# Cross-attention and routed feed-forward: the last step of odd batches on GpSimd, first roots for four batches at once, and a later normalisation

## The chip, the cores and the metric

The kernel runs on one core of one Trainium2 chip. The metric is the device time of one execution in microseconds (us). Its engines are called here by their names and, in rows of the profile, PE (TensorE), PEld (TensorE's weight loads), DVE (VectorE), ACT (ScalarE), POOL (GpSimd) and SP (SyncE, the DMA queue).

## The reference, cut to what matters

x and ctx are 128 batches of 128 rows by 256 columns, float32.

```python
def reference(x, ctx, Wq, bq, Wkv, bkv, Wo, bo, w_router, w_block):
    h = layernorm(x)                                   # (x - m) / sqrt(v + 1e-5), over 256 columns
    q, k, v = h @ Wq + bq, ctx @ Wkv[:, :256] + bkv[:256], ctx @ Wkv[:, 256:] + bkv[256:]
    attn = softmax(q_h @ k_h.T / 4)                    # 16 heads of 16
    x1 = x + (attn @ v_h) @ Wo + bo
    z = layernorm(x1)
    top = top_k(z @ w_router, 96 of 128 rows)          # in each batch
    u = z;  u[top] = gelu(z[top] @ w_block)            # the other rows keep z
    return x1 + u
```

## The kernel before, in words

One batch (128 x 256, rows on the partitions) is the unit of work. After a prologue each engine runs a hand-written loop over s, and one pass ("slot s") works on several batches at different stages. The engines are tied by semaphores only: each executes its list in program order, and a wait holds everything behind it on that engine. Four engines carry one list each.

TensorE in slot s (functions of the same names): `scores(s)` (L329), `transpose_inputs(s + 5)` (L358, of the normalised x, `xhat`, and of ctx), `values(s - 1)` and the queries or keys of a pair (both through L287), the router's two small transposes once in eight slots (`candidates` L473 where s = 4 mod 8, `keep_columns` L480 where s = 0 mod 8), `projection(s - 2)` (L294), a wait for `xhat` of batch s + 6, `block_product(s - 4)` (L294), then a wait for `v_pad` of batch s - 1 (`scaled_values_ready`), `transpose_x1(s - 3)` (L374) and `attention(s - 1)` (L394). In slots 20 to 119 the wait for `v_pad` stands ahead of `transpose_x1`.

ScalarE in slot s: `attention_copy(s - 2)`, `gelu_tanh(s - 7)`, `inputs_high(s + 5)` (L569), and the 16 exponentials of batch s (L558).

VectorE in slot s: the copy of transposed x1, the statistics of both norms (L705, L710, L694, L699), the four maxima (L671), `values_and_bias` (L764), `inputs_low` (L723), `inverse_sums(s - 1)` (L716, it makes `recip`), queries or keys and their bias, `residual` (L688), the router's steps (L791 to L813, in five of eight slots), `final(s - 16)` (L829) and `product_scaled(s - 4)` (L776). `final` is the last step of a batch: z_sb = z_sb * half_keep + x1_sb, where z_sb holds twice the gelu, half_keep is 0.5 for kept rows and 0 for the others, and x1_sb already holds what x1 + u has beside the gelu (`unprocessed`).

GpSimd in slot s, in this order: `normalise(s + 7)` (L984), `rstd1_of_pair(s + 9)` in odd slots (L972 variance + eps, L973 negated mean, L975 power -0.5) or `rstd2_of_pair(s - 4)` in even slots (L1015, L1017), `gelu_square(s - 5)` (L1033), `values_over_sums(s - 1)` (L1004, it makes `v_pad` and waits for `recip`), `scale_and_shift` once in eight slots (L1072, L1073), `unprocessed(s - 16)` (L1082), `gelu_factor(s - 5)` (L1043), `gelu_sum(s - 7)` (L1057), `input_and_bias(s + 4)` (L993), `gelu_cubic(s - 5)` (L1050) and `gelu_product(s - 7)` (L1064).

SP in slot s: in odd slots the eight q_eo transfers of a pair, the store of a pair (`store(s - 17)`, when both finals are done) and `load_x(s + 13)`; in even slots `load_c(s + 8)`.

x, x1 and z are kept in rings of 16 batches, `xhat` and the gelu's intermediate in rings of four. The last batches run through an epilogue written out by hand. The order of GpSimd's loop is:

```python
            for s in range(4, B):
                sure = 20 <= s < B - 1
                normalise(s + 7, sure)
                rstd1_of_pair(s + 9)
                rstd2_of_pair(s - 4)
                gelu_square(s - 5, sure)
                values_over_sums(s - 1, sure)
```

## Time and profile before

| | |
|---|---|
| median of 3 runs | 929.75 us (929.29 to 930.64) |
| the profiled execution | 928.47 us, span 926.7 us |
| granted TensorE clock, mean | 0.986 of full speed |
| TensorE, weight loads | busy 891.2 us (96%), 756.0 us (82%) |
| VectorE | busy 872.8 us (94%) |
| ScalarE | busy 876.0 us (95%) |
| GpSimd | busy 796.2 us (86%) |
| DMA | 25.8% of the span of 16 engines |

The page gives busy time and, for each group of instructions, how long the engine idled before it and what ended the wait. The timeline gives single instructions: start, length, engine, line, tiles written and read, and in brackets the idle time before with its releaser. Numbers in tile names are left out there, so x_sb stands for x_sb and x1_sb, rstd for rstd1 and rstd2, and so on. Instructions on one engine can overlap their neighbours by some hundredths, so what one costs its queue is best read from its start to the next start.

### The profile page before, as it was taken

To read this page: it belongs to the slowest core of one execution; us is meant where nothing else is said; L and a number is where in the kernel's file an instruction comes from. 1 tells how busy PE (TensorE), PEld (TensorE's weight loads), DVE (VectorE), ACT (ScalarE), POOL (GpSimd) and SP (SyncE) were. 2 spreads that over 40 slices of the span, in tenths; PEclk is the share of its full clock that TensorE was granted. 3 is DMA by queue.
4 is the path that set the end of the run, shared out by engine and by line. 5 is a ranking of instruction groups with operands and counts; after the bars stand their busy time and mean duration, and the time that the engine had idled before them with its cause. 6 is when DMAs were issued, how large, how long until landed. Compare 5 with 4: busy or idle time off the path is not lost. (4 is left out here: it accounts for less than half of the span.)

```text
span 926.7 us, 30985 instructions
## 1 busy us (share of the span) xinstructions
PE 891.2 (96%) x10296; PEld 756.0 (82%) x10296; DVE 872.8 (94%) x2318; ACT 876.0 (95%) x4499; POOL 796.2 (86%) x1488
## 2 busy tenths in 40 slices
PE   6899999999999999999999999999999999999972
PEld 5688888888888888888888888888888888888861
DVE  4799999999999999999999999999999999999887
ACT  2899999999999999999999999999999999999983
POOL 4367879999999999899999989999999999998865
PEclk7999999999999999999999999999999999999997
DMA  5312222222232232232232223223223223221102
GB/s 171 90 50 62 67 65 59 87 76 72 86 93 56 84 92 59 84 92 63 81 89 74 73 87 93 55 86 92 58 84 92 64 79 89 72 63 53 48 23 92
DMA packets 71232, 70.71 MB, mean 76 GB/s; under 512 B 12192, under 2 KB 62880, under 8 KB 71072
## 3 DMA queue, kind: packets, MB, share of 16 engines
q1 hardware_dynamic: 71072, 68.73, 25.8%
q8 instruction: 82, 1.34, 0.6%
q14 instruction: 78, 0.64, 0.2%
HBM read 35.13 MB, written 16.78 MB: 56 GB/s over the span
## 5 line engine op out<-in xcount | busy, mean ns | idle before, releaser
L558 ACT ACTIVATE e_sb<-ps_s,neg_max 128x128 f32<-128x128 f32 x2048 | 717.1, 409 | 8.5 <-DVE neg_max L671 7.9
L558 ACT ACTIVATION_READ_ACCUMULATOR e_sb<-ps_s,neg_max 128x1 f32 x2048 | 511.1, 250 | 0.0
L671 DVE TENSOR_REDUCE neg_max<-ps_s 128x4 f32<-128x512 f32 x512 | 328.9, 663 | 32.6 <-PE ps_s L329 32.6
L329 PE MATMUL ps_s<-q_eo,k_sb 32*128 32x256 f32 x2048 | 147.6, 402 | 6.1 <-DMA q_eo<-q_raw 3.7
L394 PE MATMUL ps_a<-e_sb,v_pad 128*32 128x128 f32 x4096 | 138.4, 276 | 2.2 <-DVE x_sb L688 1.6
L294 PE MATMUL ps_a<-w_o_sb,o_sb 128*128 128x256 f32 x512 | 133.2, 382 | 2.0 <-DVE v_sb L764 1.9
L294 PE MATMUL ps_t<-w_z_sb,xt_sb 128*128 128x258 f32 x512 | 132.7, 381 | 1.3 <-DVE z_sb L776 1.3
L1004 POOL TENSOR_TENSOR v_pad<-v_sb,recip 128x256 f32<-128x256 f32 x128 | 79.4, 621 | 58.9 <-DVE recip L716 54.4
L394 PEld LDWEIGHTS ps_a<-e_sb,v_pad 128*32 128x32 f32 x4096 | 104.1, 109 | 24.0 <-issue 21.5
L329 PEld LDWEIGHTS ps_s<-q_eo,k_sb 32*128 32x128 f32 x2048 | 93.0, 185 | 34.6 <-ACT e_sb L558 18.8
L993 POOL TENSOR_TENSOR x_sb<-x_sb,bo_sb 128x256 f32<-128x256 f32 x128 | 114.7, 897 | 0.2
L294 PEld LDWEIGHTS ps_t<-w_z_sb,xt_sb 128*128 128x128 f32 x512 | 97.3, 191 | 15.3 <-issue 1.8
L294 PEld LDWEIGHTS ps_a<-w_o_sb,o_sb 128*128 128x128 f32 x512 | 88.2, 189 | 10.0 <-issue 2.5
L569 ACT CAST t_hi<-ps_t 128x512 fp32r<-128x512 f32 x127 | 74.5, 587 | 20.9 <-PE ps_t L358 15.9
L1050 POOL TENSOR_TENSOR g_sb<-g_sb,z_sb 128x256 f32<-128x256 f32 x128 | 90.7, 708 | 0.3
L723 DVE TENSOR_TENSOR t_lo<-ps_t,t_hi 128x512 fp32r<-128x512 f32 x127 | 85.9, 676 | 0.9 <-ACT t_hi L569 0.7
L287 PE MATMUL ps_a<-w_v_hi,t_hi 128*128 128x256 f32 x256 | 83.9, 328 | 1.7 <-ACT o_sb L577 1.5
L1064 POOL TENSOR_TENSOR z_sb<-g_sb,z_sb 128x256 f32<-128x256 f32 x121 | 82.5, 682 | 0.0
L287 PE MATMUL ps_q<-t_hi,w_q_hi 128*128 128x256 f32 x256 | 73.6, 288 | 4.0 <-DVE t_lo L723 2.4
L1033 POOL TENSOR_TENSOR g_sb<-z_sb 128x256 f32<-128x256 f32 x123 | 75.3, 612 | 0.3 <-DVE z_sb L776 0.3
L287 PE MATMUL ps_q<-t_hi,w_q_lo 128*128 128x256 f32 x256 | 73.1, 285 | 0.0
L287 PE MATMUL ps_q<-t_lo,w_q_hi 128*128 128x256 f32 x256 | 73.1, 285 | 0.0
(92 smaller groups left out, 2195.1 us busy)
## 6 DMA issues: line engine op xcount, KB each, us to landing
x_sb<-in_x SPq DMA_DIRECT2D x64, 256.0 KB, 3.0
c_sb<-in_ctx SPq DMA_DIRECT2D x64, 256.0 KB, 3.2
q_eo<-q_raw SPq DMA_DIRECT2D x512, 32.0 KB, 2.0
out<-z_sb SPq DMA_DIRECT2D x64, 256.0 KB, 2.4
z_sb<-in_L_xattn_Wkv SPq DMA_DIRECT2D x2, 256.0 KB, 5.3
...
```

The lines of the kernel that those rows point to most:

```text
L287: last = nc.tensor.matmul(dst, lhs(a, c), rhs(b, c), start=(c == 0 and n == 0), stop=(c == C - 1 and n == len(terms) - 1))
L294: last = nc.tensor.matmul(dst, lhs(c), rhs(c), start=(c == 0), stop=(c == C - 1))
L329: mm = nc.tensor.matmul(ps_s[:, bank(b, j), c, :, :], k_sb[rows, r2, c, h * T:(h + 1) * T], q_eo[rows, r2, :, c, h, :], start=True, stop=True)
L394: mm = nc.tensor.matmul(ps_attn[32 * j:32 * j + 32, c * T:(c + 1) * T], v_pad[:, b % 2, c * J + j, par:par + 2, :].rearrange("p a d -> p ( ...
L558: last = nc.scalar.activation(e_sb[:, b % 4, j, c, par, :], ps_s[:, bank(b, j), c, par, :], ACT.Exp, bias=neg_max[:, b % 4, h:h + 1], accu ...
L671: nc.vector.tensor_reduce(neg_max[:, b % 4, :].rearrange("p (c j q) -> p j c q", c=C, j=J)[:, j, :, :], ps_s[:, bank(b, j), :, :, :], AX.X ...
L723: nc.vector.tensor_tensor(t_lo[part].rearrange("p k c t -> p (k c) t"), inputs_bank(b)[:, :].rearrange("p (n t) -> p n t", t=T), t_hi[part ...
L993: nc.gpsimd.tensor_tensor(x_sb[:, b % R, :], x_sb[:, b % R, :], bo_sb[:, :], ALU.add).then_inc(xb_ready, 1)
L1004: nc.gpsimd.tensor_tensor(v_pad[:, b % 2, :, 0:3:2, :], v_sb[:, b % 2, :].rearrange("p (g q d) -> p g q d", q=2, d=D), recip[:, b % 4, :]. ...
L1033: nc.gpsimd.tensor_tensor(g_sb[:, b % 4, :], z_sb[:, b % R, 0:E], z_sb[:, b % R, 0:E], ALU.mult).then_inc(square_ready, 1)
L1050: nc.gpsimd.tensor_tensor(g_sb[:, b % 4, :], g_sb[:, b % 4, :], z_sb[:, b % R, 0:E], ALU.mult).then_inc(cubic_ready, 1)
L1064: nc.gpsimd.tensor_tensor(z_sb[:, b % R, 0:E], g_sb[:, b % 4, :], z_sb[:, b % R, 0:E], ALU.mult).then_inc(gelu_ready, 1)
```

## The change

There are three edits, all of them about GpSimd's list.

1. `final` of the odd batches 5 to 111 (54 of them) leaves VectorE. GpSimd does it in two steps in slot b + 16: `final_scaled` multiplies z_sb by the column half_keep, and four steps later `final_sum` adds x1_sb. The store of a pair waits for both engines.
2. First roots (1 / sqrt(variance + eps) of x) are taken for four batches at once from batch 16 on: `variance1` ahead of `values_over_sums` and `root1` behind it, in slots 9, 13, 17, ..., 117. Before, it was two batches in every odd slot.
3. `normalise` subtracts the mean as it stands, so that the negation is dropped, and it works on batch s + 6 in place of s + 7.

```diff
@@ sb tiles @@
-        eps_sb = sb("eps_sb", [P, 2])
-        minus_half = sb("minus_half", [P, 2])
+        eps_sb = sb("eps_sb", [P, 4])
+        minus_half = sb("minus_half", [P, 4])
-        neg_m1 = sb("neg_m1", [P, R])
...
+        FINAL_ON_POOL = tuple(range(5, B - 16, 2))
+
+        def finals_on_pool(b):
+            return sum(1 for n in FINAL_ON_POOL if n <= b)
@@ SP, store @@
-                    sp.wait_ge(final_ready, upto(b + 1))
+                    sp.wait_ge(final_ready, upto(b + 1) - finals_on_pool(b + 1))
+                    if b + 1 in FINAL_ON_POOL:
+                        sp.wait_ge(final_pool_ready, finals_on_pool(b + 1))
@@ VectorE, final @@
-                if has(b):
+                if has(b) and b not in FINAL_ON_POOL:
@@ GpSimd @@
+            def final_scaled(b):
+
+                if b in FINAL_ON_POOL:
+                    g, k, r = (b // GROUP) % 2, b % GROUP, b % R
+                    nc.gpsimd.tensor_scalar(z_sb[:, r, 0:E], z_sb[:, r, 0:E], half_keep[:, g, k:k + 1], None,
+                                            ALU.mult).then_inc(scaled_ready, 1)
+
+            def final_sum(b):
+
+                if b in FINAL_ON_POOL:
+                    pool.wait_ge(u_ready, upto(b))
+                    pool.wait_ge(scaled_ready, finals_on_pool(b))
+                    nc.gpsimd.tensor_tensor(z_sb[:, b % R, 0:E], z_sb[:, b % R, 0:E], x1_sb[:, b % R, :],
+                                            ALU.add).then_inc(final_pool_ready, 1)
+
+            def variance1(b, n):
+
+                if b % n == 0 and has(b):
+                    r = slice(b % R, b % R + n)
+                    pool.wait_ge(mv1_ready, upto(b + n - 1))
+                    nc.gpsimd.tensor_tensor(ve1[:, r], mv1[:, r, 1], eps_sb[:, 0:n], ALU.add).then_inc(ve1_ready, n)
+
+            def root1(b, n):
+
+                if b % n == 0 and has(b):
+                    r = slice(b % R, b % R + n)
+                    pool.wait_ge(ve1_ready, upto(b + n - 1))
+                    nc.gpsimd.tensor_tensor(rstd1[:, r], ve1[:, r], minus_half[:, 0:n], ALU.pow).then_inc(rstd1_ready, n)
+
             def rstd1_of_pair(b):
...
+                variance1(b, 2)
+                root1(b, 2)
...
-                    nc.gpsimd.tensor_scalar(xhat[:, b % 4, :], x_sb[:, r, :], neg_m1[:, r:r + 1], rstd1[:, r:r + 1],
-                                            ALU.add, ALU.mult).then_inc(xhat_ready, 1)
+                    nc.gpsimd.tensor_scalar(xhat[:, b % 4, :], x_sb[:, r, :], mv1[:, r, 0:1], rstd1[:, r:r + 1],
+                                            ALU.subtract, ALU.mult).then_inc(xhat_ready, 1)
...
-            normalise(10)
-
             for s in range(4, B):
                 sure = 20 <= s < B - 1
-                normalise(s + 7, sure)
-                rstd1_of_pair(s + 9)
+                normalise(s + 6, sure)
                 rstd2_of_pair(s - 4)
                 gelu_square(s - 5, sure)
+                if s == 5:
+                    variance1(14, 2)
+                if s >= 9:
+                    variance1(s + 7, 4)
                 values_over_sums(s - 1, sure)
+                if s == 5:
+                    root1(14, 2)
+                if s >= 9:
+                    root1(s + 7, 4)
                 scale_and_shift(s - 16)
                 unprocessed(s - 16, sure)
                 gelu_factor(s - 5)
+                final_scaled(s - 16)
                 gelu_sum(s - 7)
                 input_and_bias(s + 4)
                 gelu_cubic(s - 5)
+                final_sum(s - 16)
                 gelu_product(s - 7)
```

GpSimd's list from `v_pad` of slot 65 on, before (x1_sb is the residual, g_sb the gelu's intermediate, ve2 and rstd2 the second root):

```order
L1004 TENSOR_TENSOR v_pad<-v_sb,recip 128x8x2x16 [waits recip_ready]
L1082 TENSOR_SCALAR x1_sb<-x1_sb,alpha,beta 128x256 [waits beta_ready]
L1043 TENSOR_SCALAR g_sb<-g_sb 128x256 [waits square_ready]
L1057 TENSOR_SCALAR g_sb<-g_sb 128x256 [waits tanh_ready]
L993 TENSOR_TENSOR x_sb<-x_sb,bo_sb 128x256 [waits xhat_ready]
L1050 TENSOR_TENSOR g_sb<-g_sb,z_sb 128x256 [waits factor_ready]
L1064 TENSOR_TENSOR z_sb<-g_sb,z_sb 128x256 [waits gelu_sum_ready]
L984 TENSOR_SCALAR xhat<-x_sb,neg_m1,rstd1 128x256 [waits rstd1_r]
L1015 TENSOR_TENSOR ve2<-mv2,eps_sb 128x2 [waits mv2_r]
L1017 TENSOR_TENSOR rstd2<-ve2,minus_half 128x2 [waits ve2_r]
L1033 TENSOR_TENSOR g_sb<-z_sb 128x256 [waits z_ready]
L1004 TENSOR_TENSOR v_pad<-v_sb,recip 128x8x2x16 [waits recip_ready]
```

The same place now (the last two rows above, square and next `v_pad`, follow behind L1048, the second root's power):

```order
L1035 TENSOR_TENSOR v_pad<-v_sb,recip 128x8x2x16 [waits recip_ready]
L1001 TENSOR_TENSOR rstd1<-ve1,minus_half 128x4 [waits ve1_r]
L1113 TENSOR_SCALAR x1_sb<-x1_sb,alpha,beta 128x256 [waits beta_ready]
L1074 TENSOR_SCALAR g_sb<-g_sb 128x256 [waits square_ready]
L978 TENSOR_SCALAR z_sb<-z_sb,half_keep 128x256
L1088 TENSOR_SCALAR g_sb<-g_sb 128x256 [waits tanh_ready]
L1024 TENSOR_TENSOR x_sb<-x_sb,bo_sb 128x256 [waits xhat_ready]
L1081 TENSOR_TENSOR g_sb<-g_sb,z_sb 128x256 [waits factor_ready]
L986 TENSOR_TENSOR z_sb<-z_sb,x1_sb 128x256 [waits scaled_ready,u_ready]
L1095 TENSOR_TENSOR z_sb<-g_sb,z_sb 128x256 [waits gelu_sum_ready]
L1015 TENSOR_SCALAR xhat<-x_sb,mv1,rstd1 128x256 [waits rstd1_r]
L1046 TENSOR_TENSOR ve2<-mv2,eps_sb 128x2 [waits mv2_r]
```

Three instructions are new between the two `v_pad`: L1001 (only where s = 1 mod 4), L978 and L986 (in every odd slot from 21 on).

TensorE's list around the wait for `v_pad` in slot 66 is the same before and after; here it is of the change (L301 is `block_product`, L381 `transpose_x1`, L401 `attention`, L336 the next `scores`):

```order
L301 MATMUL ps_t<-w_z_sb,xt_sb 128x258 [waits t_lo_ready,c_in4,xhat_ready]
L301 MATMUL ps_t<-w_z_sb,xt_sb 128x258
L381 MATMUL ps_q<-ident,x1_sb 128x128 [waits k_ready,v_pad_ready]
L381 MATMUL ps_q<-ident,x1_sb 128x128
L401 MATMUL ps_a<-e_sb,v_pad 32x128 [waits x1_ready]
L401 MATMUL ps_a<-e_sb,v_pad 32x128 x15
L336 MATMUL ps_s<-q_eo,k_sb 128x256 [waits exp_ready1]
```

The wait for `v_pad_ready` stands at the transpose of x1, ahead of attention and of the next scores. On VectorE the list of an odd slot is as before without L829.

## Rows read from the trace of the kernel before

**Rows 1.** The page, part 1: busy time, share of the span, instructions.

```profile
PE 891.2 (96%) x10296; PEld 756.0 (82%) x10296; DVE 872.8 (94%) x2318; ACT 876.0 (95%) x4499; POOL 796.2 (86%) x1488
```

**Rows 2.** Timeline, TensorE's weight loads: start us, length us, what, [idle before, releaser].

```profile
469.36 0.74 PEld L329 LDWEIGHTS ps_s<-q_eo,k_sb 32*128 32x128 f32 x16 [0.20 <-issue]
...
476.13 0.74 PEld L329 LDWEIGHTS ps_s<-q_eo,k_sb 32*128 32x128 f32 x16 [0.20 <-ACT e_sb L558]
...
481.38 0.36 PEld L374 LDWEIGHTS ps_q<-ident,x_sb 128*128 128x128 f32 x2
...
482.92 0.74 PEld L329 LDWEIGHTS ps_s<-q_eo,k_sb 32*128 32x128 f32 x16 [0.20 <-ACT e_sb L558]
...
524.15 0.74 PEld L329 LDWEIGHTS ps_s<-q_eo,k_sb 32*128 32x128 f32 x16 [0.20 <-issue]
```

**Rows 3.** Timeline of an early slot: weight loads of the scores, and v_pad on GpSimd.

```profile
85.54 0.74 PEld L329 LDWEIGHTS ps_s<-q_eo,k_sb 32*128 32x128 f32 x16 [0.20 <-ACT e_sb L558]
...
92.32 0.74 PEld L329 LDWEIGHTS ps_s<-q_eo,k_sb 32*128 32x128 f32 x16 [0.20 <-ACT e_sb L558]
...
89.30 0.62 POOL L1004 TENSOR_TENSOR v_pad<-v_sb,recip 128x256 f32<-128x256 f32 x1 [1.16 <-DVE recip L716]
```

**Rows 4.** Timeline, VectorE in slots 65 and 66.

```profile
475.07 0.48 DVE L829 SCALAR_TENSOR_TENSOR z_sb<-z_sb,half_keep,x_sb 128x256 f32<-128x256 f32 x1
475.47 0.42 DVE L694 BATCH_NORM_STATS2 st<-x_sb 128x6 f32<-128x256 f32 x1
...
477.42 1.29 DVE L671 TENSOR_REDUCE neg_max<-ps_s 128x4 f32<-128x512 f32 x2 [0.27 <-PE ps_s L329]
...
479.57 0.24 DVE L716 RECIPROCAL recip<-sums 128x16 f32<-128x16 f32 x1
```

**Rows 5.** Timeline, GpSimd from v_pad of slot 65 to v_pad of slot 66.

```profile
473.11 0.62 POOL L1004 TENSOR_TENSOR v_pad<-v_sb,recip 128x256 f32<-128x256 f32 x1
473.72 0.56 POOL L1082 TENSOR_SCALAR x_sb<-x_sb,alpha,beta 128x256 f32<-128x256 f32 x1
474.35 0.40 POOL L1043 TENSOR_SCALAR g_sb<-g_sb 128x256 f32<-128x256 f32 x1
...
475.20 0.94 POOL L993 TENSOR_TENSOR x_sb<-x_sb,bo_sb 128x256 f32<-128x256 f32 x1
476.11 0.72 POOL L1050 TENSOR_TENSOR g_sb<-g_sb,z_sb 128x256 f32<-128x256 f32 x1
...
477.51 0.55 POOL L984 TENSOR_SCALAR xhat<-x_sb,neg_m,rstd 128x256 f32<-128x256 f32 x1
478.04 0.18 POOL L1015 TENSOR_TENSOR ve<-mv,eps_sb 128x2 f32<-128x2 f32 x1
478.36 0.70 POOL L1017 TENSOR_TENSOR rstd<-ve,minus_half 128x2 f32<-128x2 f32 x1
479.03 0.61 POOL L1033 TENSOR_TENSOR g_sb<-z_sb 128x256 f32<-128x256 f32 x1
479.89 0.62 POOL L1004 TENSOR_TENSOR v_pad<-v_sb,recip 128x256 f32<-128x256 f32 x1 [0.25 <-DVE recip L716]
```

**Rows 6.** Timeline, weight loads of the scores of slots 70 and 71.

```profile
503.37 0.31 PEld L329 LDWEIGHTS ps_s<-q_eo,k_sb 32*128 32x128 f32 x8 [0.20 <-ACT e_sb L558]
...
510.25 0.53 PEld L329 LDWEIGHTS ps_s<-q_eo,k_sb 32*128 32x128 f32 x12 [0.20 <-issue]
```

**Rows 7.** Timeline, GpSimd: the bias sum of slot 68.

```profile
495.56 0.73 POOL L993 TENSOR_TENSOR x_sb<-x_sb,bo_sb 128x256 f32<-128x256 f32 x1
```

**Rows 8.** Timeline, GpSimd: first roots and v_pad of slot 67.

```profile
484.63 0.19 POOL L972 TENSOR_TENSOR ve<-mv,eps_sb 128x2 f32<-128x2 f32 x1
...
485.66 0.61 POOL L1033 TENSOR_TENSOR g_sb<-z_sb 128x256 f32<-128x256 f32 x1
486.67 0.62 POOL L1004 TENSOR_TENSOR v_pad<-v_sb,recip 128x256 f32<-128x256 f32 x1 [0.41 <-DVE recip L716]
```

**Rows 9.** Timeline, GpSimd near the end: the power of one column.

```profile
909.38 0.56 POOL L1024 TENSOR_TENSOR rstd<-ve,minus_half 128x1 f32<-128x1 f32 x1
```

More of the change, by code:

```diff
@@ L193, in cross_attention_routed_ffn @@
         final_ready = sem("final_ready")
+        scaled_ready, final_pool_ready = sem("scaled_ready"), sem("final_pool_ready")
         block = ctx.enter_context(nc.Block())
@@ L965, in _ @@
             pool.wait_ge(v_pad_zero, 1)
-            def rstd1_of_pair(b):
-                if b % 2 == 0 and has(b):
-                    r = slice(b % R, b % R + 2)
-                    pool.wait_ge(mv1_ready, upto(b + 1))
-                    nc.gpsimd.tensor_tensor(ve1[:, r], mv1[:, r, 1], eps_sb[:, :], ALU.add).then_inc(ve1_ready, 2)
-                    nc.gpsimd.tensor_scalar(neg_m1[:, r], mv1[:, r, 0], -1.0, None, ALU.mult)
-                    pool.wait_ge(ve1_ready, upto(b + 1))
-                    nc.gpsimd.tensor_tensor(rstd1[:, r], ve1[:, r], minus_half[:, :], ALU.pow).then_inc(rstd1_ready, 2)
+            def final_scaled(b):
[19 more added lines that the diff above has]
+                    nc.gpsimd.tensor_tensor(rstd1[:, r], ve1[:, r], minus_half[:, 0:n], ALU.pow).then_inc(rstd1_ready, n)
+            def rstd1_of_pair(b):
+                variance1(b, 2)
+                root1(b, 2)
             def normalise(b, settled=False):
@@ L1014, in rstd2_of_pair @@
                     pool.wait_ge(mv2_ready, upto(b + 1))
-                    nc.gpsimd.tensor_tensor(ve2[:, r], mv2[:, r, 1], eps_sb[:, :], ALU.add).then_inc(ve2_ready, 2)
+                    nc.gpsimd.tensor_tensor(ve2[:, r], mv2[:, r, 1], eps_sb[:, 0:2], ALU.add).then_inc(ve2_ready, 2)
                     pool.wait_ge(ve2_ready, upto(b + 1))
-                    nc.gpsimd.tensor_tensor(rstd2[:, r], ve2[:, r], minus_half[:, :], ALU.pow).then_inc(rstd2_ready, 2)
+                    nc.gpsimd.tensor_tensor(rstd2[:, r], ve2[:, r], minus_half[:, 0:2], ALU.pow).then_inc(rstd2_ready, 2)
             def rstd2_of_one(b):
```

## The prediction, made before the changed kernel ran

> **What bounds the kernel now.** I read the busy shares first. Four engines are busy for 86% to 96% of the span [rows 1], so a share alone decides nothing. The question is which engine has no slack in the main loop, where one batch takes one pass ("slot") s. I then followed TensorE's weight loads from one first score product (L329) to the next: an ordinary slot is 6.77 to 6.79 us (469.36, 476.13, 482.92), and the eight slots to 524.15 take 54.79 [rows 2]. A bubble of 0.20 us stands ahead of the scores in every slot, whoever is named as its releaser.
>
> The proof that this pace is TensorE's own stands in the early slots. From 85.54 to 92.32, before any final step or router is running on VectorE, the slot is 6.78 too, and GpSimd sits idle 1.16 us in it ahead of v_pad [rows 3]. So slack on GpSimd and VectorE buys nothing below 6.78. In slot 66 VectorE idles as well, 0.27 us until the scores come [rows 4].
>
> GpSimd is next, since the change loads it. Its queue from v_pad of slot 65 to v_pad of slot 66 takes 479.89 - 473.11 = 6.78 us, of which 0.25 is idle, until VectorE's reciprocal [rows 5]. So it works 6.53 us. The even v_pad ends at 479.89 + 0.62 = 480.51. TensorE's transpose of x1 (L374), which must wait for it, starts at 481.38 [rows 2], 0.87 us later. A release takes about 0.08 us: the reciprocal ended at 479.57 + 0.24 = 479.81 [rows 4], v_pad began at 479.89. **So v_pad of an even slot may start 0.79 us later than it does, and no more**: a stretch from odd to even v_pad may be 6.78 + 0.79 = 7.57 us long. What is queued behind that wait on TensorE (attention, the next scores, the next transposes) moves with it one to one.
>
> **The change, part by part.**
>
> *VectorE loses 54 final steps* (batches 5 to 111, odd). One costs 475.47 - 475.07 = 0.40 us of its queue [rows 4]. VectorE isn't the bound, so this gives only what its lateness costs TensorE. I find one such place, behind the router's steps: slot 70 is 510.25 - 503.37 = 6.88 long, 0.10 above the ordinary [rows 6]. I credit it whole: 13 groups of eight x 0.10 = **-1.3 us**. The bounds are 0, and all that eight slots hold above eight ordinary ones, 54.79 - 8 x 6.78 = 0.55, that is 7.2 us; the rest of it is where TensorE has the router's two small products, so I leave it out.
>
> *GpSimd, odd slots: two steps more.* final_scaled reads one tensor and one column per partition. The nearest rows are tensor_scalar steps: 0.40 us with constants (L1043), 0.53 to the next start for normalise (L984), 0.63 for the shift (L1082) [rows 5]. I take 0.53, the same kind of operands, with the others as bounds. final_sum adds two tensors of 256, like L1050 and L1064, which take 477.51 - 476.11 = 1.40 together [rows 5]. I take 0.70, bounds 0.61 (v_pad, 473.11 to 473.72) and 0.72.
>
> *What the missing final gives back.* In this slot the bias sum L993 takes 0.94 us, begun at 475.20 while VectorE's final (two SBUF inputs) runs from 475.07; where GpSimd was first it took 0.73 [rows 4, 5, 7]. Without the final: -0.21.
>
> *GpSimd, first roots.* Gone from every odd slot are sum, negation and power, 485.66 - 484.63 = 1.03 us [rows 8]. They stood ahead of an odd v_pad, in the stretch from even to odd. In their place one slot in four has a four-column sum ahead of v_pad (0.18 like the two-column one, L1015) and **a four-column power behind v_pad, in an odd slot, so in the stretch to the tight even one**. The power took 0.70 us for two columns [rows 5] and 0.56 for one [rows 9], 0.14 a column: four are an estimated 0.98, and 0.95 to the next start, as two took 0.67 (478.36 to 479.03). Bounds: 0.67 (no dearer than two columns) and 1.37 (two of them).
>
> *The stretches.* Odd to even without the root: 6.53 - 0.21 + 0.53 + 0.70 = 7.55 us, which just fits in 7.57. With the root: 7.55 + 0.95 = 8.50, which is 0.93 too long. So in slots 22, 26, ... TensorE waits 0.93 us for v_pad. There are 25 (root and final in one slot: s = 21, 25, ..., 117): 25 x 0.93 = **+23.3 us**.
>
> *Does it catch up?* Even to odd the work was 486.67 - 479.89 - 0.41 = 6.37 and becomes 6.37 - 1.03 + 0.18 = 5.52 [rows 5, 8]. After its wait TensorE takes 1.54 us to the next scores (481.38 to 482.92), and from these to the next v_pad it is 3.75 (482.92 to 486.67) [rows 2, 8]. So the odd v_pad comes 0.62 + 0.08 + 1.54 + 3.75 = 5.99 us after the even one and GpSimd idles 0.47 before it. Its lateness ends there, but TensorE has no slack to regain its own. The idle time merely moves ahead of the odd v_pad, where it helps nobody.
>
> *Normalise a slot later.* TensorE asks for it before the block product, but on GpSimd it stands ahead of second root and square, 1.6 us before v_pad even starts, and v_pad is wanted next, at L374. So v_pad is always the later of the two. Cost 0; the cover is this order. If it went, the wait would move to the block product and not grow. Subtracting the mean is the same instruction with another operand: 0.
>
> *Stores.* An odd batch's last step now ends late in GpSimd's slot, so SP issues the store of a pair up to some 4 us later, and the load of x behind it. That load is used three slots (20 us) on, and z_sb is wanted again three slots on. Next on SP are a load of ctx used four slots on and the q_eo transfers of two slots on. Cost 0; without that cover a late landing would cost its lateness once in two slots.
>
> *The end.* GpSimd finishes slot 127 about 1.2 us later and then waits for VectorE's statistics as now: 0.
>
> **Sum.** +23.3 - 1.3 = +22.0 on the profiled execution's 928.47 us gives 950.5. The median of the runs is 1.28 above that execution (929.75), so the forecast is **951.8 us**. All bounds low: 6.32 + 0.40 + 0.61 + 0.67 = 8.00, 0.43 too long, 25 x 0.43 - 1.3 = +9.5, 939 us. All high: 9.04, 1.47 too long, and the 29 stretches without a root 0.10 too long, +38, 968 us.
>
> The Trainium skill ("GPSIMD Engine Reference", 4.1 Engine selection) sends elementwise work to VectorE and puts GpSimd at about twice its time for two-input steps. This speaks against the change; the rows here are harsher, since one step of 0.40 becomes two of together 1.23.
>
> **Rivals.**
> *Cheaper steps on GpSimd.* The two final steps together take twice VectorE's 0.40, that is 0.80, the power as estimated. The stretch is 6.32 + 0.80 + 0.95 = 8.07, the wait 0.50, the sum 12.5 - 1.3 = +11.2, **941 us**. For it: an unseen step with one column may run at L1043's 0.40. Against: final_sum alone has rows near 0.70. (It is the time that the factor of two of the page named above would give.)
> *Faster: the stretch fits.* If final_scaled, final_sum and the power stay under 7.57 - 6.32 = 1.25 us together, or TensorE does not in truth stop at L374, only VectorE's relief is left, 1.3 to 7.2 us, middle 4.3: **925.5 us**. For it: slots behind the router are longer, so VectorE does reach TensorE. Against: the low ends of the rows sum to 1.68 already, and the early slots show the pace without that load.
> *Nothing measurable.* The steps are cheap and the waits vanish in TensorE's bubbles (0.20 ahead of the scores): about 930. Against: these bubbles stand in every slot, waiting or not.
> *Much slower.* Power in proportion to columns and a dear final_scaled, so that stretches without a root overrun too: **968 us**. For it: those fit by 0.02 us only.
>
> **Chances.** Forecast (943 to 966) 0.66; cheaper steps 0.14; faster 0.08; nothing measurable 0.06; much slower 0.06. The likeliest gives the time. The range 931 to 966 takes in the first two and leaves out 0.20. A measurement of this kernel can tell about 0.2% (1.9 us) from no change: faster 0.08, same 0.06, slower 0.86.
>
> **What would show it.** In the profile after: TensorE waiting about 0.9 us for v_pad ahead of the transpose of x1 in slots 22, 26, ..., 25 times, and hardly elsewhere; a slot of about 7.7 us there and 6.78 beside it; the four-column power near 0.98 us, final_scaled near 0.55, final_sum near 0.72, the bias sum 0.73 in odd slots; GpSimd idle about 0.5 us ahead of odd v_pads and not ahead of even ones; VectorE idle more. The forecast is wrong if the even v_pad behind a root still waits for the reciprocal, or if the slots of 6.78 get shorter.

## The result, and the profile after

The changed kernel takes **1011.51 us** (median of 4 runs, 1009.19 to 1013.08). The kernel before, run beside it, takes 929.52 (928.34 to 930.64, 4 runs). The ratio is 1.0886, with an interval of 1.0865 to 1.0907. It is slower, as predicted, but by 82.0 us where 22 were forecast and 38 were the dearest case thought of.

The profiled execution took 1013.08 us, with a span of 1011.2. First the page's busy times, which answer to [rows 1]:

```profile
PE 917.6 (91%) x10296; PEld 756.3 (75%) x10296; DVE 858.7 (85%) x2264; ACT 880.3 (87%) x4499; POOL 920.9 (91%) x1476
```

GpSimd has 124.7 us more work than before (920.9 against 796.2). The prediction gave it far less: 54 x (0.53 + 0.70 - 0.21) = 55 us for the final steps, and less work for the first roots. So the question is which instructions hold the rest. The groups of instructions on GpSimd, shapes apart (line, operation, tiles, shapes, count | busy us, mean ns | idle before them):

```profile
L1015 POOL TENSOR_SCALAR xhat<-x_sb,mv,rstd 128x256 f32<-128x256 f32 x128 | 157.0, 1227 | 0.4
...
L978 POOL TENSOR_SCALAR z_sb<-z_sb,half_keep 128x256 f32<-128x256 f32 x54 | 50.3, 931 | 5.1
...
L986 POOL TENSOR_TENSOR z_sb<-z_sb,x_sb 128x256 f32<-128x256 f32 x54 | 34.5, 639 | 0.0
L1001 POOL TENSOR_TENSOR rstd<-ve,minus_half 128x4 f32<-128x4 f32 x28 | 28.8, 1028 | 0.0
```

`normalise` (L1015) takes 1.23 us; before it took 0.55 [rows 5, L984]. The prediction had its new operand at nothing and did not price its new operation. That is 128 x 0.68 = 87 us of GpSimd's time. `final_scaled` (L978) takes 0.93, against 0.53 forecast and 0.63 at most. `final_sum` (0.64) and the four-column power (1.03) are near their forecasts of 0.70 and 0.98.

The timeline of GpSimd, slot 65 (odd, with a root and a final step) to v_pad of slot 67 (start, length). These rows answer to [rows 5]:

```profile
512.51 0.63 POOL L1035 TENSOR_TENSOR v_pad<-v_sb,recip 128x256 f32<-128x256 f32 x1
513.09 1.03 POOL L1001 TENSOR_TENSOR rstd<-ve,minus_half 128x4 f32<-128x4 f32 x1
...
515.27 0.93 POOL L978 TENSOR_SCALAR z_sb<-z_sb,half_keep 128x256 f32<-128x256 f32 x1
...
519.23 1.22 POOL L1015 TENSOR_SCALAR xhat<-x_sb,mv,rstd 128x256 f32<-128x256 f32 x1
...
522.03 0.62 POOL L1035 TENSOR_TENSOR v_pad<-v_sb,recip 128x256 f32<-128x256 f32 x1
...
529.24 0.62 POOL L1035 TENSOR_TENSOR v_pad<-v_sb,recip 128x256 f32<-128x256 f32 x1 [1.11 <-DVE recip L723]
...
537.76 0.62 POOL L1035 TENSOR_TENSOR v_pad<-v_sb,recip 128x256 f32<-128x256 f32 x1
543.98 0.62 POOL L1035 TENSOR_TENSOR v_pad<-v_sb,recip 128x256 f32<-128x256 f32 x1
```

The stretch with the root is 522.03 - 512.51 = 9.52 us (forecast 8.50), the odd-to-even one without it 537.76 - 529.24 = 8.52 (forecast 7.55). The other two are 7.21, of which 1.11 idle, and 6.22 (6.37 was the work before). Four slots hold 31.47 - 1.11 = 30.36 us of work. TensorE's pace, routers included, was 54.79 / 2 = 27.4 in four slots [rows 2]. **GpSimd's total no longer fits, so there is no stretch in which it catches up.** It is now the engine that sets the pace.

The wait table of the stretch from 300 to 700 us (engine, line, what it waited for: us, times, longest):

```profile
PEld ps_q L381 <- POOL v_pad L1035: 31.0, 26, 1.5
...
PEld ps_t L301 <- POOL xhat L1015: 15.9, 13, 1.4
...
POOL v_pad L1035 <- DVE recip L723: 2.3, 2, 1.2
```

TensorE waits for GpSimd in every even slot, in half of them twice. GpSimd waits for the reciprocal only twice, in some 52 slots. The whole main loop confirms it. From slot 21 to slot 119 v_pad moves from the first to the second of these rows:

```profile
173.66 0.62 POOL L1035 TENSOR_TENSOR v_pad<-v_sb,recip 128x256 f32<-128x256 f32 x1
...
928.05 0.62 POOL L1035 TENSOR_TENSOR v_pad<-v_sb,recip 128x256 f32<-128x256 f32 x1
```

That is 754.39 us in 98 slots, 7.70 each. Before, the same slots went from 171.63 to 843.07, 671.44 us, 6.85 each. The difference is 82.95. The two profiled executions are 84.5 us apart in their spans (1011.2 and 926.7), so nearly all the lost time lies in these slots.

A part of it is TensorE's clock. After the two waits of slot 66, the table by windows (window, length, busy of PE, PEld, DVE, ACT, POOL with counts, then the granted clock) shows it at half speed:

```profile
520.50:523.00 2.50, 1.44 (x6) 0.97 (x6) 0.03 (x1) 2.11 (x13) 2.36 (x5) 0.88 0.63 203
523.00:525.20 2.20, 2.20 (x37) 1.41 (x35) 1.98 (x7) 0.00 (x0) 2.03 (x5) 0.50 0.00 0
525.20:528.00 2.80, 2.80 (x32) 2.37 (x29) 1.33 (x4) 1.44 (x5) 2.80 (x4) 0.89 0.00 0
```

0.50 is 1.2 GHz, 1.00 is 2.4 GHz. TensorE had been busy 1.44 of the 2.50 us before. The weight loads show what came ahead of it:

```profile
514.67 0.74 PEld L336 LDWEIGHTS ps_s<-q_eo,k_sb 32*128 32x128 f32 x16 [0.20 <-ACT e_sb L565]
...
520.51 0.73 PEld L301 LDWEIGHTS ps_t<-w_z_sb,xt_sb 128*128 128x128 f32 x4 [1.44 <-POOL xhat L1015]
...
522.70 0.29 PEld L381 LDWEIGHTS ps_q<-ident,x_sb 128*128 128x128 f32 x2 [1.46 <-POOL v_pad L1035]
...
525.18 1.04 PEld L336 LDWEIGHTS ps_s<-q_eo,k_sb 32*128 32x128 f32 x16 [0.38 <-issue]
```

From the transpose of x1 to the next scores it takes 525.18 - 522.70 = 2.48 us, where it took 1.54 before [rows 2]. The next reciprocal is late by it, and GpSimd idles 1.11 us at 529.24. Between 173 and 928 us there are five such places; the idle times ahead of v_pad there are 1.33, 1.21, 1.11, 1.24 and 1.09, together 5.98 us. So of the 82.95 about 6 are the clock's, and 77 are GpSimd's own work back to back.

### The profile page after: what moved, and what is told of

It is laid out like the page before. It is cut to its first block and busy times, and to the rows that moved or that the text cites. A ratio compares the mean times of both kernels' runs of the same rounds, so it can differ in the third digit from the quotient of the medians.

```text
span 1011.2 us, 30969 instructions
## 1 busy us (share of the span) xinstructions
PE 917.6 (91%) x10296; PEld 756.3 (75%) x10296; DVE 858.7 (85%) x2264; ACT 880.3 (87%) x4499; POOL 920.9 (91%) x1476
## 5 line engine op out<-in xcount | busy, mean ns | idle before, releaser
L1015 POOL TENSOR_SCALAR xhat<-x_sb,mv,rstd 128x256 f32<-128x256 f32 x128 | 157.0, 1227 | 0.4
L336 PE MATMUL ps_s<-q_eo,k_sb 32*128 32x256 f32 x2048 | 150.9, 409 | 5.6 <-DMA q_eo<-q_raw 3.4
L301 PE MATMUL ps_t<-w_z_sb,xt_sb 128*128 128x258 f32 x512 | 135.3, 386 | 20.9 <-POOL xhat L1015 19.7
L401 PE MATMUL ps_a<-e_sb,v_pad 128*32 128x128 f32 x4096 | 142.5, 281 | 2.8 <-POOL xhat L1015 0.9
L301 PE MATMUL ps_a<-w_o_sb,o_sb 128*128 128x256 f32 x512 | 133.2, 382 | 2.1 <-DVE v_sb L771 2.0
L301 PEld LDWEIGHTS ps_t<-w_z_sb,xt_sb 128*128 128x128 f32 x512 | 95.3, 190 | 43.8 <-POOL xhat L1015 29.7
L401 PEld LDWEIGHTS ps_a<-e_sb,v_pad 128*32 128x32 f32 x4096 | 106.9, 112 | 25.8 <-issue 22.0
L336 PEld LDWEIGHTS ps_s<-q_eo,k_sb 32*128 32x128 f32 x2048 | 95.1, 190 | 35.6 <-ACT e_sb L565 15.8
L836 DVE SCALAR_TENSOR_TENSOR z_sb<-z_sb,half_keep,x_sb 128x256 f32<-128x256 f32 x74 | 35.8, 492 | 83.0 <-POOL x_sb L1113 82.8
L301 PEld LDWEIGHTS ps_a<-w_o_sb,o_sb 128*128 128x128 f32 x512 | 88.2, 189 | 10.1 <-issue 2.6
L1024 POOL TENSOR_TENSOR x_sb<-x_sb,bo_sb 128x256 f32<-128x256 f32 x128 | 92.9, 727 | 0.2
L584 ACT COPY o_sb<-ps_a 128x256 f32<-128x256 f32 x128 | 55.4, 433 | 40.5 <-PE ps_a L401 40.5
L1081 POOL TENSOR_TENSOR g_sb<-g_sb,z_sb 128x256 f32<-128x256 f32 x128 | 88.6, 692 | 0.3
L381 PE MATMUL ps_q<-ident,x_sb 128*128 128x128 f32 x256 | 52.7, 288 | 39.8 <-POOL v_pad L1035 38.8
```

The source lines that it names most:

```text
L301: last = nc.tensor.matmul(dst, lhs(c), rhs(c), start=(c == 0), stop=(c == C - 1))
L336: mm = nc.tensor.matmul(ps_s[:, bank(b, j), c, :, :], k_sb[rows, r2, c, h * T:(h + 1) * T], q_eo[rows, r2, :, c, h, :], start=True, stop=True)
L401: mm = nc.tensor.matmul(ps_attn[32 * j:32 * j + 32, c * T:(c + 1) * T], v_pad[:, b % 2, c * J + j, par:par + 2, :].rearrange("p a d -> p ( ...
L1015: nc.gpsimd.tensor_scalar(xhat[:, b % 4, :], x_sb[:, r, :], mv1[:, r, 0:1], rstd1[:, r:r + 1], ALU.subtract, ALU.mult).then_inc(xhat_ready, 1)
L1024: nc.gpsimd.tensor_tensor(x_sb[:, b % R, :], x_sb[:, b % R, :], bo_sb[:, :], ALU.add).then_inc(xb_ready, 1)
L1081: nc.gpsimd.tensor_tensor(g_sb[:, b % 4, :], g_sb[:, b % 4, :], z_sb[:, b % R, 0:E], ALU.mult).then_inc(cubic_ready, 1)
```

## The experiments

Experiments that ran together on a chip share the runs of the kernel before: 929.34 us (13 runs) for e0 to e3, 929.20 (15 runs) for e4 to e7, 927.96 (15 runs) for e8 to e10.

### What makes a GpSimd step slow

Three ideas were open for the 1.23 and the 0.93. **A**: the pair of operations decides. **B**: the place of the mean in memory does, since it is now read out of pairs (mean, variance). **C**: a step with a lone column or with one operation is slow as such, and a subtraction is no slower than an addition.

**e0_forms**: the kernel before, with 22 steps on idle data put at GpSimd's end, each reading 128x256 and writing to a tile of its own.

```diff
+            FORMS = [(c0, c1, ALU.add, ALU.mult), (c0, c1, ALU.subtract, ALU.mult), (c0, c1, ALU.mult, ALU.add),
+                     (mv1[:, 0, 0:1], c1, ALU.add, ALU.mult), (c0, None, ALU.mult, None), (c0, 0.0, ALU.mult, ALU.add),
+                     (c0, 1.0, ALU.mult, ALU.mult), (c0, None, ALU.add, None), (0.5, None, ALU.mult, None),
+                     (0.5, 1.0, ALU.mult, ALU.add), (c0, c1, ALU.mult, ALU.subtract)]
+                for n, (p, q, o0, o1) in enumerate(FORMS):
```

> The kernel before with 22 tensor_scalar steps on GpSimd behind its last step, on idle data (11 forms, each twice, 128 x 256). The changed kernel's normalise took 1.23 us where it took 0.55, and its final_scaled 0.93. Theory A (the operations decide): add+mult and mult+add with two columns 0.55 us, whichever tile the column comes from; subtract+mult 1.23; mult alone with a column 0.93; mult+add with a column and a constant 0.45 to 0.6. Theory B (the operand decides): add+mult with the column out of the pair tile mv1 also 1.23, and subtract+mult with columns out of alpha and beta 0.55. Theory C (any step with a lone column or a bypassed second operation is slow): mult and add alone 0.93, subtract+mult no longer than add+mult.

Measured, the timeline of GpSimd, second round, in the order of that list:

```profile
929.87 0.55 POOL L1162 TENSOR_SCALAR scr<-x_sb,alpha,beta 128x256 f32<-128x256 f32 x1
930.40 1.23 POOL L1162 TENSOR_SCALAR scr<-x_sb,alpha,beta 128x256 f32<-128x256 f32 x1
931.61 0.55 POOL L1162 TENSOR_SCALAR scr<-x_sb,alpha,beta 128x256 f32<-128x256 f32 x1
932.15 0.55 POOL L1162 TENSOR_SCALAR scr<-x_sb,mv,beta 128x256 f32<-128x256 f32 x1
932.68 0.93 POOL L1160 TENSOR_SCALAR scr<-x_sb,alpha 128x256 f32<-128x256 f32 x1
933.59 0.47 POOL L1162 TENSOR_SCALAR scr<-x_sb,alpha 128x256 f32<-128x256 f32 x1
934.03 0.48 POOL L1162 TENSOR_SCALAR scr<-x_sb,alpha 128x256 f32<-128x256 f32 x1
934.49 0.93 POOL L1160 TENSOR_SCALAR scr<-x_sb,alpha 128x256 f32<-128x256 f32 x1
935.38 0.85 POOL L1160 TENSOR_SCALAR scr<-x_sb 128x256 f32<-128x256 f32 x1
936.21 0.40 POOL L1162 TENSOR_SCALAR scr<-x_sb 128x256 f32<-128x256 f32 x1
936.61 1.22 POOL L1162 TENSOR_SCALAR scr<-x_sb,alpha,beta 128x256 f32<-128x256 f32 x1
```

Two operations out of add and mult take 0.40 (two constants), 0.47 (column and constant) or 0.55 us (two columns), in either order. One with subtract takes 1.23 as the first, 1.22 as the second. One operation alone takes 0.93 with a column and 0.85 with a constant. The mean read in place costs nothing (fourth row, 0.55). So A holds and B falls. Half of C holds: the multiplication alone takes 0.46 us longer than with a second operation that changes nothing (fifth and sixth row). Its other half falls, since the subtraction is slow in a pair too. Why the engine is slower for these is not known from any run here.

**e1_before_subtract**: the kernel before, with the changed `normalise` alone.

```diff
-                    nc.gpsimd.tensor_scalar(neg_m1[:, r], mv1[:, r, 0], -1.0, None, ALU.mult)
...
-                    nc.gpsimd.tensor_scalar(xhat[:, b % 4, :], x_sb[:, r, :], neg_m1[:, r:r + 1], rstd1[:, r:r + 1],
-                                            ALU.add, ALU.mult).then_inc(xhat_ready, 1)
+                    nc.gpsimd.tensor_scalar(xhat[:, b % 4, :], x_sb[:, r, :], mv1[:, r, 0:1], rstd1[:, r:r + 1],
+                                            ALU.subtract, ALU.mult).then_inc(xhat_ready, 1)
```

> The kernel before with one edit: normalise subtracts the mean out of mv1, the negation is gone; order and everything else as before. If the edit alone carries the 1.23 us: GpSimd's two slots take 6.53 + 0.68 and 6.37 - 0.20 + 0.68, together 14.06 us against 13.56 of TensorE, so in the loop with finals a pair of slots is 0.5 us longer and the whole about 955 us (945 to 962). If the slow normalise in the changed kernel comes of something else in it (its place in the slot, neighbours): 929 to 930.5 us and 0.55 us an instruction. Were the operand harmless and only the shared port at fault, the early slots would show 0.55 too.

Measured: 966.83 us (966.18 to 968.38), ratio 1.0407 (1.039 to 1.0425). **This one operand and operation, with nothing else changed, costs 37.5 us.** Its group, and the wait between 300 and 700:

```profile
L982 POOL TENSOR_SCALAR xhat<-x_sb,mv,rstd 128x256 f32<-128x256 f32 x128 | 158.2, 1237 | 0.4
```

```profile
PEld ps_q L373 <- POOL v_pad L1002: 31.6, 55, 0.8
```

TensorE waits in every one of the 55 slots between 300 and 700, and GpSimd never waits for a reciprocal there. That is more than expected (955, and 962 at most). The expectation took GpSimd's work in two slots from one place, 6.53 + 6.37 = 12.90. Over slots 21 to 119 of the kernel before it is 13.2: two slots take 13.70 there, and GpSimd idles 24.8 us ahead of v_pad in the 98 slots, 0.25 each. So a slot has 0.68 more work, 0.10 less for the negation, and 0.25 of slack to take it up. The 0.33 left are 32 us in 98 slots. The other steps add little: `gelu_factor` takes 608 ns on the mean (408 before), as VectorE's final step now runs beside it, but the bias sum is rid of that neighbour and takes 732 (897 before). Together they are 0.035 us dearer a slot, 3 us in all. These 35 us are what slots 21 to 119 lost (35.7).

**e2_negated_in_place**: the kernel before, but the negated mean is written back into mv1 and read from there.

```diff
-                    nc.gpsimd.tensor_scalar(neg_m1[:, r], mv1[:, r, 0], -1.0, None, ALU.mult)
+                    nc.gpsimd.tensor_scalar(mv1[:, r, 0], mv1[:, r, 0], -1.0, None, ALU.mult)
...
-                    nc.gpsimd.tensor_scalar(xhat[:, b % 4, :], x_sb[:, r, :], neg_m1[:, r:r + 1], rstd1[:, r:r + 1],
+                    nc.gpsimd.tensor_scalar(xhat[:, b % 4, :], x_sb[:, r, :], mv1[:, r, 0:1], rstd1[:, r:r + 1],
                                             ALU.add, ALU.mult).then_inc(xhat_ready, 1)
```

> The kernel before, with the negated mean written back into mv1 (stride of two) and read from there by the same add and mult. Theory A (operations): normalise 0.55 us, 929.5 us within 1.5. Theory B (operand out of the pair tile): normalise 1.23 us and about 955 us or more.

Measured: 930.59 us (928.30 to 931.73, 10 runs), ratio 1.001 (1.0001 to 1.0019); `normalise` takes 556 ns. It reads the mean where e1 does and has the operations of before, and 36 of e1's 37.5 us are gone. The operation is the cause.

### The change with cheap steps

**e3_after_with_add**: the changed kernel, with the negation back (four columns, 0.24 us, behind `variance1`) and `normalise` as add and mult.

```diff
                     nc.gpsimd.tensor_tensor(ve1[:, r], mv1[:, r, 1], eps_sb[:, 0:n], ALU.add).then_inc(ve1_ready, n)
+                    nc.gpsimd.tensor_scalar(neg_m1[:, r], mv1[:, r, 0], -1.0, None, ALU.mult)
...
-                    nc.gpsimd.tensor_scalar(xhat[:, b % 4, :], x_sb[:, r, :], mv1[:, r, 0:1], rstd1[:, r:r + 1],
-                                            ALU.subtract, ALU.mult).then_inc(xhat_ready, 1)
+                    nc.gpsimd.tensor_scalar(xhat[:, b % 4, :], x_sb[:, r, :], neg_m1[:, r:r + 1], rstd1[:, r:r + 1],
+                                            ALU.add, ALU.mult).then_inc(xhat_ready, 1)
```

> The changed kernel with the negation back (four columns at once behind variance1) and normalise by add and mult; finals and roots for four as in the change. By the chain (a stretch odd to even over 7.57 us is paid in full): with the root 6.32 + 0.90 + 0.62 + 1.00 = 8.84, without it 7.84, so 1.27 + 0.27 = 1.54 us in four slots, 25 x 1.54 - 1.3: about 967 us (958 to 975). Rival, only GpSimd's total counts (27.9 us in four slots against 27.4 of TensorE): about 943 us (938 to 950).

Measured: **957.08 us** (955.75 to 958.17), ratio 1.0296 (1.0281 to 1.0312), 54.4 us below the changed kernel. GpSimd's timeline around the stretch with a root, and the wait between 300 and 700:

```profile
513.52 0.62 POOL L1037 TENSOR_TENSOR v_pad<-v_sb,recip 128x256 f32<-128x256 f32 x1
...
522.37 0.62 POOL L1037 TENSOR_TENSOR v_pad<-v_sb,recip 128x256 f32<-128x256 f32 x1
```

```profile
PEld ps_q L382 <- POOL v_pad L1037: 19.0, 14, 1.4
```

The stretch is 8.85 and TensorE waits 14 times 1.36 us, once in four slots; the waits in the other even slots are gone, and of those for xhat one of 0.2 us is left. The clock stays at 1.00 throughout the main loop. This is the pattern that was predicted, with `final_scaled` still at 0.93.

The time is just below the range of the expectation (958 to 975). That had a loss of 0.27 us in each stretch without a root as well. These stretches are 7.82 to 7.84 us long here, over the 7.57 allowed, and yet no wait shows. The 7.57 was read in slot 66. In each even slot without a root TensorE has one of the router's small transposes, and there the transpose of x1 comes later. In the kernel before, v_pad of slot 67 starts at 486.67 [rows 8], and slot 68 goes on with:

```profile
495.05 0.36 PEld L374 LDWEIGHTS ps_q<-ident,x_sb 128*128 128x128 f32 x2
```

So a stretch from slot 67 to 68 may be 495.05 - 0.08 - 0.62 - 486.67 = 7.68 us long, and one from 71 to 72 likewise 7.82 (v_pad 514.10, transpose 522.62).

**e4_two_columns**: e3, with `final_scaled` as multiply by the column and add a column of zeros.

```diff
-                    nc.gpsimd.tensor_scalar(z_sb[:, r, 0:E], z_sb[:, r, 0:E], half_keep[:, g, k:k + 1], None,
-                                            ALU.mult).then_inc(scaled_ready, 1)
+                    nc.gpsimd.tensor_scalar(z_sb[:, r, 0:E], z_sb[:, r, 0:E], half_keep[:, g, k:k + 1], zero_col[:, :],
+                                            ALU.mult, ALU.add).then_inc(scaled_ready, 1)
```

> The kernel of the run before (changed kernel, negation back, normalise by add and mult), and final_scaled written as mult by half_keep and add of a column of zeros, the pair of operations that took 0.55 us with two columns where mult alone took 0.93. So this is the change with its two slow instructions in a fast form. Chain theory: the stretch with the root is 8.86 - 0.38 = 8.48, TensorE waits 0.9 us in 25 slots, the others fit: 25 x 0.88 - 1.3, about 950 us (946 to 954). If only GpSimd's total counts (27.2 us in four slots against 27.4): 929 to 931. If final_scaled still takes 0.93, the pair of operations isn't what decides: 957.

Measured: **945.10 us** (943.96 to 946.47), ratio 1.017 (1.0157 to 1.0184), 12.0 below e3 and 1 us below the expected range. The step's group, and TensorE's weight loads over one slot with a wait:

```profile
L981 POOL TENSOR_SCALAR z_sb<-z_sb,half_keep,zero_col 128x256 f32<-128x256 f32 x54 | 30.0, 556 | 5.3
```

```profile
511.14 0.74 PEld L338 LDWEIGHTS ps_s<-q_eo,k_sb 32*128 32x128 f32 x16 [0.20 <-ACT e_sb L567]
...
517.24 0.20 PEld L383 LDWEIGHTS ps_q<-ident,x_sb 128*128 128x128 f32 x2 [0.88 <-POOL v_pad L1039]
518.62 0.74 PEld L338 LDWEIGHTS ps_s<-q_eo,k_sb 32*128 32x128 f32 x16 [0.20 <-issue]
```

This kernel is the change as the prediction had it: `normalise` at 0.56 and `final_scaled` at 0.56. Its stretch with the root is 8.44 us (forecast 8.50) and the wait 0.88 (forecast 0.93). But the slot, which is slot 70, takes 518.62 - 511.14 = 7.48, and it took 6.88 before [rows 6]: 0.60 more. Slot 66 takes 7.47 here (483.21 to 490.68) and took 6.79 [rows 2]: 0.68 more. After the wait TensorE needs 518.62 - 517.24 = 1.38 to the next scores, not the 1.54 of [rows 2]: its two weight loads go in 0.20 us, and 0.36 where they follow the product without a pause. So some 0.2 of each wait is absorbed, and in slot 70 the 0.10 too by which that slot was longer than others. Of the 25 slots 13 are like slot 70 and 12 like slot 66: 13 x 0.60 + 12 x 0.68 = 16.0; 15.9 were measured.

**e10_only_scale_mended**: the changed kernel with e4's `final_scaled`, and `normalise` still subtracting. It asks what the same 0.37 is worth when GpSimd has no slack at all. The diff is that of e4.

> The changed kernel with final_scaled in the fast two-column form and nothing else mended: normalise still subtracts (1.23 us). There GpSimd has no slack in any slot, so every 0.37 us of the 54 scales counts: 1011.5 - 54 x 0.37 = 991.5 us (988 to 996). If the chain's arithmetic of single stretches held with slack between, as from e3 to e4, only 12 us come off: 999.5.

Measured: 988.60 us (987.78 to 989.98), ratio 1.0652 (1.0637 to 1.0666): 22.9 us below the changed kernel. Every one of the 54 steps counts, 54 x 0.37 = 20. The other 3 are the clock's: it falls twice in the main loop instead of five times, and GpSimd idles 2.6 us ahead of v_pad there, not 6.0. With slack (e3 to e4) it was 12.0: 0.40 us in each of the 13 slots like slot 70 and 0.57 in each of the 12 like slot 66. In these the odd v_pad ahead is late already in e3 (3.90 us behind its slot's first scores, 3.76 in e4). So a step's price depends on whether the queue around it has slack. The waits of e10 in 300 to 700:

```profile
PEld ps_q L382 <- POOL v_pad L1037: 27.8, 27, 1.5
...
PEld ps_t L302 <- POOL xhat L1017: 10.1, 14, 1.1
```

### Where the rest of the loss sits

**e5_root_ahead**: e4 with the four-column power ahead of v_pad, and so in the even-to-odd stretch.

```diff
-                values_over_sums(s - 1, sure)
...
                     root1(s + 7, 4)
+                values_over_sums(s - 1, sure)
```

> As e4_two_columns, with the four-column power ahead of v_pad in its slot, where GpSimd idled. Chain theory: the stretch from even to odd grows to 5.9 + 1.0 = 6.9, so the odd v_pad behind an even one that was 0.7 late is itself 0.7 to 0.8 late, and the next stretch of 7.46 makes it 1.4, 0.6 over the allowance: 25 x 0.6 - 1.3, about 942 us (937 to 947). Total theory: no difference from e4_two_columns. If the power's place is all that was wrong with the order: 929.

Measured: **932.87 us** (931.88 to 934.89), ratio 1.0042 (1.0026 to 1.0059): 12.2 us less from the place of 28 instructions. In 300 to 700:

```profile
PEld ps_q L383 <- POOL v_pad L1039: 5.5, 14, 0.7
```

The four stretches are 7.46, 6.97 or 6.72, 7.46 and 5.81, together 27.70 or 27.45, where four slots took 27.4 before [rows 2]. That nearly fits, and the waits left are mostly 0.33 to 0.38. The power stands where there was slack for it. The expectation (942, 937 to 947) was too dear: it had the odd v_pad 0.7 to 0.8 us late, and in slot 69 it is 0.46 late (4.23 us behind the slot's first scores, 3.77 in e4).

**e6_roots_alone**: e3 with no final step on GpSimd. That leaves the roots for four and the later `normalise`.

```diff
-        FINAL_ON_POOL = tuple(range(5, B - 16, 2))
+        FINAL_ON_POOL = ()
```

> Roots for four batches (with the negation) and the later normalise of the change, but every final on VectorE as before. Chain theory: odd to even 6.53 + 1.03 = 7.56 us, just inside 7.57 to 7.6, so nothing waits: 928.5 to 931 us. If the allowance is smaller than I read it, some 0.1 us in each of 28 slots: 932.

Measured: 932.72 us (932.15 to 932.80), ratio 1.0035 (1.0022 to 1.0047). The expectation named 932 for some 0.1 us in each of 28 slots. The number was met, but by luck: the loss lies elsewhere. Of the 4.2 us that slots 21 to 119 lose, 3.5 are in two slots of each eight. Slot 70 takes 505.45 to 512.47, 7.02 (6.88 before), and slot 71 takes 6.97 (6.78 before). A late v_pad is not the cause. The rows, from VectorE's final step just ahead of slot 70 on:

```profile
505.00 0.72 DVE L837 SCALAR_TENSOR_TENSOR z_sb<-z_sb,half_keep,x_sb 128x256 f32<-128x256 f32 x1
...
510.17 0.62 POOL L1037 TENSOR_TENSOR v_pad<-v_sb,recip 128x256 f32<-128x256 f32 x1
510.23 0.66 DVE L759 TENSOR_TENSOR k_sb<-ps_q,bk_sb 128x512 f32<-128x512 f32 x1
...
511.01 0.20 PEld L382 LDWEIGHTS ps_q<-ident,x_sb 128*128 128x128 f32 x2 [0.20 <-POOL v_pad L1037]
```

The same step in the kernel before:

```profile
507.79 0.66 DVE L751 TENSOR_TENSOR k_sb<-ps_q,bk_sb 128x512 f32<-128x512 f32 x1
```

The transpose of x1 waits for k_sb as well as for v_pad. The profile names v_pad, but the transpose starts 0.84 us behind its start, against 0.67 where v_pad really is the last (e4), and 0.12 behind the end of k_sb. VectorE's k_sb starts 4.78 us behind the slot's first scores and did so at 4.42 before (507.79 - 503.37 [rows 6]). So VectorE is 0.36 later. Its final step ahead of this takes 0.72 us, where it took 0.46 before (at 502.81). It also starts some 0.1 later behind its neighbour, as it needs GpSimd's `unprocessed`, which now stands behind the power and ends at 504.96. In slot 71 TensorE waits for ScalarE's o_sb (0.17 us, ahead of L295); what makes that late was not followed.

That two steps beside each other get longer shows in slot 68 of e6:

```profile
497.64 0.73 POOL L1026 TENSOR_TENSOR x_sb<-x_sb,bo_sb 128x256 f32<-128x256 f32 x1
...
497.82 0.83 DVE L837 SCALAR_TENSOR_TENSOR z_sb<-z_sb,half_keep,x_sb 128x256 f32<-128x256 f32 x1
```

VectorE's final takes 0.83 where it took 0.48 [rows 4]. GpSimd's bias sum started first here and took 0.73; in [rows 5] VectorE was first, and then that sum took 0.94. Whoever starts second pays. The Trainium skill ("SBUF — State Buffer", on the shared port pair) says that VectorE with two inputs in SBUF and GpSimd take a common port pair for a whole instruction, and that the one that comes second is blocked; these two pairs of rows agree with it. That such a collision makes VectorE late in slot 70 is read from the trace and was not tested by itself.

**e7_finals_left_out**: the kernel before without the last step of the odd batches 5 to 111, on any engine. This leaves out that part of the computation, and the store of a pair waits for the gelu product instead.

```diff
-                if has(b):
+                if has(b) and b not in LEFT_OUT:
```

> The kernel before with the final step of the odd batches 5 to 111 left out (the store waits for the gelu's product in its place), so VectorE is relieved and GpSimd has nothing more to do. If TensorE bounds the loop (6.78 us a slot whatever VectorE does): 1.3 us less, 927 to 929.5. If VectorE sets the pace in part: 0.40 us off half the slots, down to ScalarE's floor, 915 to 922.

Measured: 928.59 us (927.71 to 930.01, 11 runs), ratio 0.9993 (0.9984 to 1.0002). VectorE is 54 x 0.40 = 22 us lighter and the time does not move: the relief is 0.6 us, if any. Slot 70, which the prediction credited with 0.10, still takes 6.93 (503.61 to 510.54), so its 0.10 does not come from the final step alone. VectorE's wait for the scores in 300 to 700 is now the following, and was 7.9 us in 30 times before:

```profile
DVE neg_max L678 <- PE ps_s L336: 15.9, 37, 0.7
```

So the whole idea of the change, a lighter VectorE, has nothing to win while TensorE sets the pace.

**e8_finals_alone**: e4 with first roots and `normalise(s + 7)` as before, so that the moved final steps stand alone.

```diff
-                normalise(s + 6, sure)
+                normalise(s + 7, sure)
+                rstd1_of_pair(s + 9)
...
-                    root1(s + 7, 4)
```

> The finals of the odd batches on GpSimd in the fast two-column form, but the first roots in pairs and normalise in its old place, as before. Chain theory: odd to even 7.45 us, inside the allowance alone; but even to odd is 6.37, so GpSimd works 13.82 us in two slots against 13.56 (13.7 with the router's extras), its lateness adds up and TensorE waits a little in nearly every even slot: about 942 us (937 to 946), with no odd v_pad waiting for the reciprocal. If only a single stretch counts and not the sum of both: 928 to 930.

Measured: 936.85 us (934.85 to 937.71), ratio 1.009 (1.0076 to 1.0104), just below the expected 937 to 946. The odd-to-even stretch is 7.43, under the allowance of 7.57, and yet TensorE waits in 20 of some 29 even slots, 0.34 to 0.53 us:

```profile
PEld ps_q L383 <- POOL v_pad L1039: 8.2, 20, 0.5
```

The reason is the other stretch. With the pair's roots back it is 6.42, and 7.43 + 6.42 = 13.85 is 0.15 more than two slots took before (54.79 / 4 = 13.70 [rows 2]). Over 54 pairs of slots that is 8.1 us; 8.9 were measured. GpSimd is full again, if only just, and its total decides.

**e9_every_fourth_final**: e5 with every fourth final on GpSimd (7, 11, 15, ...), the version that the runs pointed to as the best.

```diff
-        FINAL_ON_POOL = tuple(range(5, B - 16, 2))
+        FINAL_ON_POOL = tuple(range(7, B - 16, 4))
```

> As e5_root_ahead (power ahead of v_pad, fast forms), but only the finals of batches 7, 11, 15, ... on GpSimd, in the slots without a root. Chain theory: stretches 7.45 and 6.53 odd to even, both inside the allowance, the power's odd v_pad 0.3 us late at most: no waits, and VectorE relieved: 928.3 to 930 us, so as before and 3 to 4 us under e5_root_ahead. If VectorE's finals keep colliding with GpSimd's first two-input step as in e6_roots_alone: 931 to 933.

Measured: 927.39 us (926.32 to 929.10, 11 runs), ratio 0.9991 (0.9982 to 1.0000). TensorE waits for no v_pad between 300 and 700, and GpSimd idles there:

```profile
POOL v_pad L1039 <- DVE recip L725: 17.6, 14, 1.4
```

It is as fast as the kernel before: 0.6 us under it, less than 0.1%, with an interval that reaches 1, and a little under the 928.3 to 930 expected. No version measured here beats that kernel by what can be told.

## Why the prediction was wrong in size

The 82 us, taken apart by e4 and e3. The differences are those of the medians; they add up to 82.3, as the kernel before took 929.2 beside e4 and 929.5 beside the changed kernel.

| from | to | us | what |
|---|---|---|---|
| before, 929.2 | e4, 945.1 | 15.9 | the moved steps, the roots for four and the order, all in their cheap forms |
| e4, 945.1 | e3, 957.1 | 12.0 | `final_scaled` as one operation |
| e3, 957.1 | after, 1011.5 | 54.4 | `normalise` with a subtraction |

**The step that failed** is the line "Subtracting the mean is the same instruction with another operand: 0". It is 0.68 us dearer, 128 times. The instruction had the same name in the list and in the profile, and I priced the name. I looked at what the operand costs and not at the operation. The mean's place costs next to nothing (e2: 556 ns, and 1.2 us in the whole kernel); the subtraction costs the rest (e1, e0). It stood outside the sum and outside the range, so that no bound could take it in. The case "much slower" (968) held a dear power and a dear `final_scaled`, and nothing of this.

**final_scaled** was mis-sized: 0.53 with bounds 0.40 and 0.63, measured 0.93, worth 12 to 23 us. My three rows for the bounds (L1043, L984, L1082) were all of two operations; a step of one was nowhere among them. I took "fewer operands" for "no dearer".

**Does it catch up?** It said that GpSimd idles 0.47 us ahead of an odd v_pad and that its lateness ends there. This held in e4 (0.51 idle at 508.12, 0.37 at 522.38) and failed in the changed kernel, whose four slots of work are 30.4 us for 27.4. Then every microsecond on GpSimd counts and not only those in the tight stretch.

**The chain of the argument** held once the steps cost what they were given (e4): an allowance of 7.57; a stretch of 8.44 for 8.50; a wait of 0.88 for 0.93, once in four slots at L383. The term of +23.3 came out as about 16, since some 0.2 of each wait is absorbed by TensorE's next loads, and the 0.10 of slot 70 with it. This is a piece of the rival "waits vanish in TensorE's bubbles", though in another place than it named. The other terms: power 1.03 (0.98), final_sum 0.64 (0.70), bias sum 0.73 (0.73). The relief of 1.3 has no ground in the runs: with the finals left out it is 0.6 us, within the noise, and slot 70 is no shorter (e7). The allowance of 7.57 holds for slot 66 and not for every even slot; it is 7.68 and 7.82 in slots 68 and 72 (e3). So the case "all bounds high" put a loss on 29 stretches that fit.

**Normalise a slot later: 0.** In the changed kernel waits for xhat do appear (1.44 us), but v_pad stayed the later of the two, and where `normalise` is cheap (e3) none are left. Its place was not tried alone: with roots for four batches made in slot s itself, batch s + 7 has none yet at the slot's start.

**The predicted range** (931 to 966) holds e4 and e3 but not the changed kernel. On the two-engine split the page "GPSIMD Engine Reference" (4.1 Engine selection) of the Trainium skill gives about twice VectorE's time for two-input steps. The final step went from 0.40 us to 0.56 + 0.64 in its cheap form, three times as much, and to 0.93 + 0.64 as written. No factor of this kind tells 0.55 from 1.23 for one instruction.
